# The bias of a first product as one value a partition, and its last multiplication on VectorE

## What is computed

```python
z = jax.nn.silu(xf @ sw1 + sb1) * (xf @ sw3 + sb3) @ sw2 + sb2
```

## Time and profile before

| | before |
|---|---|
| time, median of 3 runs | 1276.95 us (1274.19 to 1278.73) |
| the profiled execution | 1279.9 us, its span 1277.7 us |
| mean granted clock of PE | 0.934 of full speed |
| PE busy | 1099.5 us (86%) |
| DVE busy | 867.2 us (68%) |
| POOL busy | 840.7 us (66%) |
| ACT busy | 703.4 us (55%) |

### The profile page before, as it was taken

How to read it: one execution, slowest core, us unless ns; L and a number is a source line. 1 busy time by engine, 2 the same in 40 slices (tenths; PEclk the granted TensorE clock), 3 DMA queues, 4 the chain that set the end, 5 groups by cost and what they waited for, 6 DMA issues and landing times.

```text
span 1277.7 us, 26879 instructions
## 1 busy us (share of the span) xinstructions
PE 1099.5 (86%) x8520; PEld 711.3 (56%) x8520; DVE 867.2 (68%) x2283; ACT 703.4 (55%) x1569; POOL 840.7 (66%) x984
## 2 busy tenths in 40 slices
PE   1479989999999999999999999999866999999900
PEld 1344555655656565565656656566334788888700
DVE  4386778777787776777778777777222666666676
ACT  0115666565656656565665666666621555555534
POOL 4544558677777767777777776665664466666667
PEclk9768999999999999999999999999887999999955
DMA  4322223313143231323323133223312354454366
GB/s 88 120 80 88 80 62 118 99 54 103 56 122 98 77 101 54 101 69 124 96 65 103 55 104 108 71 75 81 107 44 81 89 157 124 120 156 123 97 212 187
DMA packets 104681, 126.16 MB, mean 99 GB/s; under 512 B 17422, under 2 KB 85344, under 8 KB 99936
## 3 DMA queue, kind: packets, MB, share of 16 engines
q1 hardware_dynamic: 91638, 104.54, 27.9%
q0 software_dynamic: 8704, 18.11, 4.0%
q10 hardware_dynamic: 4202, 1.81, 0.5%
HBM read 78.06 MB, written 45.42 MB: 97 GB/s over the span
## 4 chain that ended last, share of the span: by engine, by line
PE 72%; DVE 15%; issue 3%; DMA 2%; POOL 2%; ACT 1%; SPq 1%; POOLq 0%; DVEq 0%; ACTq 0%
PE heads_ps L1474 11%; PE wide L1502 10%; PE score L1464 10%; PE wide L1624 7%; PE wide L1439 4%; DVE mx L1276 4%; PE wide L1504 4%; PE score L1452 3%; PE wide L1605 3%; PE wide L1606 3%; PE score L1596 2%; PE wide L1535 2%; DVE chosen L1123 2%; PE wide L1622 2%; PE misc L1482 2%
## 5 line engine op out<-in xcount | busy, mean ns | idle before, releaser
L946 ACT ACTIVATE values<-score 128x512 f32<-128x512 f32 (+1 forms) x704 | 370.0, 556 | 199.9 <-PE score L1464 194.1
L1276 DVE TENSOR_REDUCE mx<-wide 128x2 f32<-128x1024 f32 (+3 forms) x384 | 387.6, 1040 | 85.5 <-PE wide L1504 84.8
L833 POOL TENSOR_SCALAR_AFFINE_SELECT values<-values 128x512 f32<-128x512 f32 x256 | 163.8, 643 | 169.0 <-ACT values L946 166.8
L1502 PE MATMUL wide<-qk 72*128 72x512 bf16 (+3 forms) x1024 | 248.8, 310 | 14.1 <-DVE mx L1276 6.0
L1464 PE MATMUL score<-qk 75*128 75x512 bf16 (+3 forms) x1024 | 237.3, 305 | 10.1 <-DMA qk<-mparts 6.2
L878 POOL DMA_INDIRECT token_scratch<-spread,e_id x144 | 137.9, 958 | 96.4 <-issue 74.5
L1504 PE MATMUL wide<-maskneg,identb 128*128 128x128 bf16 x1024 | 201.1, 225 | 0.0
L1474 PE MATMUL heads_ps<-values 128*32 128x512 f32 (+3 forms) x2048 | 176.1, 444 | 0.2 <-issue 0.2
L822 POOL DMA_INDIRECT sorted_scratch<-zr,places x128 | 129.9, 1015 | 56.4 <-DVE places L1217 19.1
L1464 PEld LDWEIGHTS score<-qk 75*128 75x128 bf16 x1024 | 88.0, 99 | 123.2 <-ACT values L946 51.7
L1502 PEld LDWEIGHTS wide<-qk 72*128 72x128 bf16 x1024 | 102.2, 100 | 90.8 <-DVE mx L1276 26.1
(11 more groups left out here) (196 smaller groups left out, 2003.2 us busy)
## 6 DMA issues: line engine op xcount, KB each, us to landing
qk<-parts_scratch SPq DMA_DIRECT2D x192, 192.0 KB
parts_scratch<-spread SPq DMA_DIRECT2D x16, 768.0 KB, 8.3
qk<-sorted_scratch SPq DMA_DIRECT2D x144, 66.0 KB
front<-token_scratch SPq DMA_DIRECT2D x16, 512.0 KB, 3.8
xt<-attn_x SPq DMA_DIRECT2D x16, 256.0 KB, 8.5
xr<-attn_x SPq DMA_DIRECT2D x16, 256.0 KB, 8.9
x_scratch<-z SPq DMA_DIRECT2D x16, 256.0 KB, 6.7
shared_scratch<-s_out SPq DMA_DIRECT2D x16, 256.0 KB
```

Of the source, the lines that this page charges most:

```text
L833: nc.gpsimd.affine_select(out=prob[n][:, :, 0:P], in_=prob[n][:, :, 0:P], compare_op=ALU.is_ge, fill=0.0, base=0, pattern=[[0, HG], [1, P] ...
L946: nc.scalar.activation(free_ap(prob[kb][:, hs_[0], :], [[1, N * len(hs_)]]), score[SCORE_RING.buffer(b, step)][:, 0:N * len(hs_)], ACT.Exp ...
L1276: nc.vector.tensor_reduce(mx[:, h0:h0 + len(hs_), j:j + 1], src, axis=AX.X, op=ALU.max).then_inc(p1_max, 1)
L1502: nc.tensor.matmul(o, q4[e][0:ROWS, h, j * P:(j + 1) * P], k4[e][0:ROWS, h, 0:L], start=True, stop=False)
```

## The change

The bias of the first product is no longer a product. ACT's tanh adds half of it (`sb1_half`, one value a partition), and G on DVE adds the whole of it (`sb1_col`) to bank 0. G multiplies by `s_g` now, and so waits for ACT's second copy and not for its tanh; H multiplies by (s_th + 1). H moves from POOL to DVE, and to other places in the lists: H0 from before mask0.2 to behind p0, H1 from behind `second` to behind O1, H2 from behind rX to behind p13. U0, U1, U2, G0, G1 and G2 stay where they are. The buffer of U is free when G and ACT's second copy have read it.

```diff
-    "chosen@-2 H0 mask0.2 v0.0 s0.7 s0.8 d0 G0 Y U0 p0 s0.9 s0.10 K p1 place mask0.3 ..."
+    "chosen@-2 mask0.2 v0.0 s0.7 s0.8 d0 G0 Y U0 p0 H0 s0.9 s0.10 K p1 place mask0.3 ..."
-    "... O1@0 stats residual s1.9 p5 p6 heads0 ... second H1 v2.0 ... p12 U2 s2.10 G2 p13 s3.0 rX s3.1 H2 d3 ..."
+    "... O1@0 H1 stats residual s1.9 p5 p6 heads0 ... second v2.0 ... p12 U2 s2.10 G2 p13 H2 s3.0 rX s3.1 d3 ..."
...
             elif user.what == "U":
-                eng.wait_ge(s_silu, c * NCH + user.n + 1)
+                eng.wait_ge(s_up_gated, c * NCH + user.n + 1)
                 eng.wait_ge(s_gate_biased, c * NCH + user.n + 1)
...
-                    elif step.what == "H":
-                        f = (b * NCH + n) % 2
-                        m = CH[n][1]
-                        pool.wait_ge(s_silu, b * NCH + n + 1)
-                        pool.wait_ge(s_gate_biased, b * NCH + n + 1)
-                        if n == 0:
-                            wait(pool, s_down, b)
-                        nc.gpsimd.tensor_tensor(s_aT[n], s_h[f][0:m], s_g[f][0:m], ALU.mult).then_inc(s_gated, 1)
...
-                        nc.scalar.activation(s_th[f][0:m], unit[0:m, 0, :], ACT.Tanh, scale=0.5).then_inc(s_tanh, 1)
+                        nc.scalar.activation(s_th[f][0:m], unit[0:m, 0, :], ACT.Tanh, scale=0.5,
+                                             bias=sb1_half[0:m, n:n + 1]).then_inc(s_tanh, 1)
...
-                        dve.wait_ge(s_tanh, b * NCH + n + 1)
-                        nc.vector.scalar_tensor_tensor(out=s_h[f][0:m], in0=s_th[f][0:m], scalar=1.0,
-                                                       in1=wide[WIDE_RING.buffer(b, UPS[n])][0:m, 0, :],
-                                                       op0=ALU.add, op1=ALU.mult).then_inc(s_silu, 1)
+                        dve.wait_ge(s_gate_biased, b * NCH + n + 1)
+                        nc.vector.scalar_tensor_tensor(out=s_h[f][0:m], in0=wide[WIDE_RING.buffer(b, UPS[n])][0:m, 0, :],
+                                                       scalar=sb1_col[0:m, n:n + 1], in1=s_g[f][0:m],
+                                                       op0=ALU.add, op1=ALU.mult).then_inc(s_up_gated, 1)
+                    elif step.what == "H":
+                        f, m = (b * NCH + n) % 2, CH[n][1]
+                        dve.wait_ge(s_up_gated, b * NCH + n + 1)
+                        if n == 0:
+                            wait(dve, s_down, b)
+                        nc.vector.scalar_tensor_tensor(out=s_aT[n], in0=s_th[f][0:m], scalar=1.0, in1=s_h[f][0:m],
+                                                       op0=ALU.add, op1=ALU.mult).then_inc(s_gated, 1)
...
-                        nc.tensor.matmul(unit[0:m, 0, :], sb1_rows[:, at:at + m], free_ap(onesb[:], [[0, NT], [1, P]]), start=True,
-                                         stop=False)
                         for part, (w, done) in enumerate(((sw1_sb, s_up), (sw3_sb, s_gate_up))):
-                            nc.tensor.matmul(unit[0:m, part, :], w[:, at:at + m], hT[:], start=(part == 1),
+                            nc.tensor.matmul(unit[0:m, part, :], w[:, at:at + m], hT[:], start=True,
                                              stop=True).then_inc(done, 1)
```

More of the change, by code:

```diff
@@ L425, in program @@
         sb2_rows = sb("sb2_rows", [P, P], BF16)
-        sb1_rows = sb("sb1_rows", [P, 2 * INTER], BF16)
+        sb1_half = sb("sb1_half", [P, NCH])
+        sb1_col = sb("sb1_col", [P, NCH])
         bias_f = view(prob[0], F32, [WIDE])[0:E + 1]
@@ L487, in program @@
         bias_split = sem("bias_split")
-        sb3_halved = sem("sb3_halved")
+        sb13_halved = sem("sb13_halved")
         bias_in = sem("bias_in")
@@ L536, in program @@
         s_tanh = sem("s_tanh")
-        s_silu = sem("s_silu")
+        s_up_gated = sem("s_up_gated")
         s_gated = sem("s_gated")
@@ L561, in program @@
         c_stored = sem("c_stored")
-        N_FW = 16 * (6 + NCH)
+        N_FW = 16 * (6 + 2 * NCH)
         N_IDENT = 11
@@ L906, in _ @@
                 act.dma_start(k4[n][ROWS:SROWS, :, :], free_ap(onesb[0:NPART, :], [[0, NH * NT], [1, P]])).then_inc(rows_filled, 16)
[L907 to L911, removed]
             for w, s in ((sw1_sb[:], sw1), (sw3_sb[:], sw3),
@@ L918, in _ @@
                 act.dma_start(sb3_col[0:m, c:c + 1], sb3[at:at + m].rearrange("(h o) -> h o", o=1)).then_inc(f_fw, 16)
+                act.dma_start(sb1_col[0:m, c:c + 1], sb1[at:at + m].rearrange("(h o) -> h o", o=1)).then_inc(f_fw, 16)
+            act.wait_ge(rows_cleared, 5)
+            act.dma_start(bias_f[0:E, 0:INTER], b1).then_inc(bias_in, 16)
+            act.dma_start(bias_f[0:E, INTER:2 * INTER], b3).then_inc(bias_in, 16)
+            act.dma_start(bias_f[0:E, 2 * INTER:], b2).then_inc(bias_in, 16)
+            act.dma_start(bias_f[E:E + 1, 2 * INTER:], row(sb2)).then_inc(bias_in, 16)
             act.dma_start(sorted_d[E * CAP:, :].rearrange("(n p) c -> p n c", p=P),
@@ L923, in body @@
                 if i == 0:
-                    act.wait_ge(bias_kept, 16 * 3 * NPART)
+                    act.wait_ge(bias_kept, 16 * 2 * NPART)
                 for step in (FRONT if i < 0 else STEPS if i < B else REST):
@@ L937, in body @@
                             act.dma_start(sb2_rows[r:r + 1, :], bias_parts[E:E + 1, r, 2 * INTER:]).then_inc(bias_kept, 16)
-                            act.dma_start(sb1_rows[r:r + 1, :], bias_parts[E:E + 1, r, 0:2 * INTER]).then_inc(bias_kept, 16)
                     elif step.what == "s":
@@ L972, in body @@
                         if b == 0 and n == 0:
-                            act.wait_ge(sb3_halved, NCH)
+                            act.wait_ge(sb13_halved, 2 * NCH)
                         wait(act, s_gated, b * NCH + n - 1)
-                        nc.scalar.activation(s_th[f][0:m], unit[0:m, 0, :], ACT.Tanh, scale=0.5).then_inc(s_tanh, 1)
+                        nc.scalar.activation(s_th[f][0:m], unit[0:m, 0, :], ACT.Tanh, scale=0.5,
+                                             bias=sb1_half[0:m, n:n + 1]).then_inc(s_tanh, 1)
                         act.wait_ge(s_gate_up, b * NCH + n + 1)
@@ L1060, in _ @@
                 nc.vector.memset(vext[n][:, :, :, HS:HS + 1], 1.0).then_inc(filled, 1)
-            for rows in (bias_rows, sb1_rows, sb2_rows, blk_own, bp_rows):
-                nc.vector.memset(rows[:], 0.0).then_inc(rows_cleared, 1)
+            for rows in (bias_rows[:], sb2_rows[:], blk_own[:], bp_rows[:], bias_f):
+                nc.vector.memset(rows, 0.0).then_inc(rows_cleared, 1)
             dve.wait_ge(filled, 4)
@@ L1137, in splits @@
             def splits():
-                dve.wait_ge(bias_in, 16 * 5)
+                dve.wait_ge(bias_in, 16 * 4)
                 bs = Steps(bias_step, 3)
@@ L1238, in body @@
                                 nc.vector.tensor_scalar(sb3_half[0:m, c:c + 1], sb3_col[0:m, c:c + 1], 0.5, None,
-                                                        ALU.mult).then_inc(sb3_halved, 1)
+                                                        ALU.mult).then_inc(sb13_halved, 1)
+                                nc.vector.tensor_scalar(sb1_half[0:m, c:c + 1], sb1_col[0:m, c:c + 1], 0.5, None,
+                                                        ALU.mult).then_inc(sb13_halved, 1)
                         shifted_logits(b, wide[WIDE_RING.buffer(b, GATE)])
@@ L1433, in body @@
                                 pe.wait_ge(f_fw, N_FW)
-                        if b == 0 and n == 0:
-                            pe.wait_ge(bias_kept, 16 * 3 * NPART)
-                        nc.tensor.matmul(unit[0:m, 0, :], sb1_rows[:, at:at + m], free_ap(onesb[:], [[0, NT], [1, P]]), start=True,
-                                         stop=False)
                         for part, (w, done) in enumerate(((sw1_sb, s_up), (sw3_sb, s_gate_up))):
-                            nc.tensor.matmul(unit[0:m, part, :], w[:, at:at + m], hT[:], start=(part == 1),
+                            nc.tensor.matmul(unit[0:m, part, :], w[:, at:at + m], hT[:], start=True,
                                              stop=True).then_inc(done, 1)
@@ L1444, in body @@
                         if b == 0:
-                            pe.wait_ge(bias_kept, 16 * 3 * NPART)
+                            pe.wait_ge(bias_kept, 16 * 2 * NPART)
                         score_free(pe, b, step)
```

## The result

The changed kernel took 1304.13 us (median of 4 runs, 1301.44 to 1307.83), the kernel before 1277.28 (4 runs): ratio 1.0215, 95% interval 1.018 to 1.0251. It is slower by 26.9 us, where 13.8 were forecast. The direction held, half of the size was missed, and the median lies just above the range's end of 1304. The profiled execution has a span of 1304.4 us against 1277.7, 26.7 more.

A forecast was written before the change was run, and what follows sets the result against it. PE's instruction stream was taken to set the loop's pace, with DVE's chain setting it at K. Terms -8.2 + 9.2 + 3.1 + 3.0 + 6.0 + 0.7 = +13.8 on 1276.95 gave 1291 us; range 1271 to 1304.

The forecast's parts named there:

- Removed products, -8.2: PE's stream: 38 of the 48 removed L1436 products are on the path at 0.215 us each, -8.2 us.
- Wait before rX, +9.2: PE before rX: G2 must follow ACT's gate copy, 0.66 us of new wait in each of 14 iterations, +9.2 us.
- p2 behind H0, +3.1: PE at p2: H0 delays p1's maximum on DVE, 0.40 us at full clock behind K's wait, +3.1 us.
- p9 behind H1, +3.0: PE at p9: H1 meets POOL's residual addition, about 0.5 us in six iterations with a slow stretch, +3.0 us.
- The second mask, +6.0: DVE chain before K: POOL's back-to-back masks hold up DVE's small copies, 0.6 us in ten iterations, +6.0 us.
- rival 1: Before K: DVE's small copies get in before POOL's second mask; then +7.8, about 1285 us; chance 0.20.
- near 55: Whole iteration at full clock: 54.1 us before, near 55 after; below 54.1 would make the prediction wrong.
- rival 2: Behind K: longer wait brings more half-speed stretches, four more costing some +5, about 1296 us; chance 0.10.
- The start, +0.7: Start and end of the program: start net -0.5 to +0.9, end up to 1 us, together +0.7 us.

The follow-up runs named there:

- before_no_products_filled: The kernel before without the sb1 product (output lacks that bias), with nine products of no use ahead of K's wait; ratio 0.9931.
- after_filled_wait: The changed kernel with eleven products of no use on PE ahead of its wait for `chosen` in ten iterations; ratio 1.0103.
- after_H1_later: The changed kernel with H1 behind p9's maximum on DVE and not behind O1; ratio 1.0235.
- before_H_on_DVE: The kernel before with H's 48 multiplications on DVE in the changed kernel's order of steps, bias product and G unchanged; ratio 1.0125.
- the two filled kernels: The kernel before with eight, the changed kernel with eleven products of no use ahead of K's wait; ratios 0.9956 and 1.0103.
- the second trace: The unedited changed kernel traced again, against the kernel before; ratio 1.0226, thirteen iterations in 723.6 us.

## Why the prediction was half right

**Removed products, -8.2.** Their price was right where K waits (0.40 us for two products in an iteration, by before_no_products_filled), their number too large: in the three iterations without a wait at K all three should count for 0.65, and the two that can be compared save 0.47 and 0.37. Measured: 3 to 5 us at full clock in the thirteen iterations, for 6.2. U0's product did not merely go into K's wait for nothing, as the step said. It lengthened the standstill, and the half clock grew from 20.5 to 41.0 us; that took the whole gain.

**Wait before rX, +9.2.** U2 to rX is 0.75 us longer in each iteration, 10.5 over fourteen; 0.66 was forecast. Around a step U2, against the earlier trace rows:

```profile
455.39 0.68 ACT L971 ACTIVATE s_g<-wide,sb_half 96x512 f32<-96x512 f32 x1 [0.18 <-PE wide L1438]
456.11 0.75 DVE L1215 SCALAR_TENSOR_TENSOR s_h<-wide,sb_col,s_g 96x512 f32<-96x512 f32 x1 [1.24 <-ACT s_g L971]
456.91 0.33 PE L1508 MATMUL wide<-ident,zr 128*128 128x128 f32 x1 [0.56 <-DVE s_h L1215]
```

G takes 0.73 to 0.75 us where it took 0.66 to 0.68: the 0.06 that the step bounded, for a scalar read from memory, and left at nothing.

**p2 behind H0, +3.1.** Right at full clock. In the first iteration of the changed kernel, at full clock:

```profile
201.80 0.68 DVE L1223 SCALAR_TENSOR_TENSOR s_aT<-s_th,s_h 128x512 f32<-128x512 f32 x1
202.40 1.22 DVE L1279 TENSOR_REDUCE mx<-wide 128x2 f32<-128x1024 f32 x1
```

```profile
201.94 0.39 PE L1552 MATMUL wide<-bp_rows,share 128*128 128x512 bf16 x1 [0.19 <-DVE mx L1279]
...
203.68 0.34 PE L1501 MATMUL wide<-qk 72*128 72x384 bf16 x1 [0.23 <-DVE mx L1279]
```

The 0.19 at W (L1552) is not new: it stands in the trace before as well, six times. What is new is the 0.23, and by start times p2 comes 3.52 us behind K at full clock, where 3.46 were forecast and 3.06 to 3.07 stood before, 0.06 of it from the longer G0. Of the three iterations without a wait at K, two lose 1.06 us and the first 0.54, not 0.5 each; none of the ten K's was left at full clock, so it is +2.7 for +3.1. That the half clock hides this wait was right as well: PE does not wait for a maximum at p2 in any of the ten. The dear part was the hiding.

**p9 behind H1, +3.0.** H1 met POOL's residual addition as described. H1 takes 1.24 to 1.44 us in nine of the ten iterations with half clock behind K. In one of them, DVE and then POOL:

```profile
269.03 1.31 DVE L1223 SCALAR_TENSOR_TENSOR s_aT<-s_th,s_h 128x512 f32<-128x512 f32 x1
```

```profile
268.53 1.26 POOL L853 TENSOR_TENSOR z<-z,xr 128x512 f32<-128x512 f32 x1
```

The wait of 0.40 stands at the first product of p9, in the same iteration:

```profile
275.03 0.34 PE L1501 MATMUL wide<-qk 72*128 72x384 bf16 x1 [0.40 <-DVE mx L1279]
```

It stands there in six iterations, of 0.34 to 0.68 us, 2.65 in all, for 3.0: right in number and near in size. In after_filled_wait, at full clock, H1 takes 0.67 at the ten K's and this wait never comes, so it is bound to the half clock. Two more of the ten have U1 to U2 longer by 0.9 and 1.0 us, but there PE waits for the transfer. after_H1_later shows that the 0.6 is paid elsewhere when H1 is not there.

**The second mask, +6.0.** 10 x 0.57 = 5.7, shown by moving the mask. In the changed kernel the held instruction is the comparison and not the small copies, so rival 1 was right in its letter and wrong in its number. But in before_H_on_DVE it is the subtraction into `zr`, as forecast, and K's wait is 0.43 us longer. That one mask more in a row costs the chain of K 0.4 to 0.6 us is shown twice; which instruction pays differs, and is not explained.

**Full clock together.** The prediction gave "near 55" for the iteration at full clock; it is 55.56 in after_filled_wait against 54.10: +1.46. With the clock full everywhere its own terms make -8.2 + 9.2 + 5.5 + 1.4 + 6.0 = 13.9 us (p2: ten times 0.40 and three times 0.5; p9: 0.1 in all fourteen). Of this some 15 belong to the thirteen iterations, which hold 29 of the 38 products; the two filled kernels are 17.1 apart there.

**The step that failed** is the one that carried the clock over unchanged: six slow stretches in the sum, and four more only as rival 2, with a chance of 0.10 and +5. The forecast itself made K's wait longer by 0.8 us, from 1.8 to 2.6, and treated that as a wait of 6 us. The runs show what hangs on it: ten stretches and not six, six of them twice as long, 12.8 us by the two filled kernels (10.3 with the second trace). The argument was that the same wait had been followed by both states, "so fewer is possible as well". It should have been read the other way: at 1.8 us six of ten fell, so the share was still free to rise with a longer wait. Adding 12.8 to a forecast of 13.8 gives 26.6 for the 26.9 measured. That closeness is luck: the thirteen iterations alone grew by 29.9, the products saved less and the waits cost more than forecast, and most of the 3.2 us that came back lies in a stretch that varies whatever the edit.

The range has an error of its own. Its upper end is said to be the forecast with four slow stretches more (1296) and the upper bounds at p9 (14 x 1.1 = 15.4 in place of 3.0). That makes 1308 and not 1304, and it would have held the measured time, for a reason that was not the cause: p9 stayed at 2.65.

Open: why one K is followed by half clock for twice as long as another, and why 2.01 and 2.03 us of standstill gave seven and nine. In the changed kernel the six long stretches all begin 0.3 to 0.9 us before K, while PE stands still, and the three that begin 1.8 to 2.2 us behind K are all short; one short one begins before K as well. Open too is why the second mask holds the comparison in one kernel and the subtraction in the other. The start, +0.7, can't be told: the first K came 1.25 us later here, and 196.0 to 202.7 us from the start over all runs.

## What to carry to other kernels

In this kernel a wait of TensorE, the bottleneck, had two prices, its own length and the slower clock behind it. When a change lengthens an existing wait on TensorE, count the stretches at half clock behind waits of that length in the trace before, and let them grow with it: here 7.8 us more of wait at K brought 10 to 13 us of clock, and a removed product that only lengthened the wait gained nothing. DVE at 68% is not free in the stretch where its results gate the next step: moving 0.6 us about within it only moved the wait. And ask first what makes the largest wait: one step of POOL moved out of the way of one comparison was worth 24.9 us, more than anything in the change.

## What was not expected of the hardware

- Filling a wait of TensorE with products of no use made both kernels faster: 0.9956 of the kernel before, and 1.0103 where the changed kernel stood at 1.0215.
- Half clock costs less than half of its length here: 18.8 us for 54.6 and 6.0 for 20.5, that is 0.34 and 0.29 us for each us of it. One part of the reason is seen: p2's wait for DVE, 0.4 us at full clock, is gone at half clock. The rest is not shown.
- Where POOL's instructions follow each other without a gap, a DVE comparison with two SBUF inputs (0.29 us alone) was passed over more than once. It took 2.38 us with two additions and one mask in a row, and got in behind the additions. With a second mask in the row it took 2.94 in the changed kernel and got in behind the first mask; in before_H_on_DVE it took 2.38, and a subtraction of 128x4 behind it took 0.60 for 0.15.
- DVE's operation of 128x512 took 0.06 us longer with a scalar read from SBUF (0.67 to 0.73; its operands changed places too), and a bias per partition made ACT's tanh 0.09 longer (0.59 to 0.68).
